# Both attentions of a two-layer vision tower: value products of two key tiles at a time, with other PSUM banks, drains and clears around them

## The reference, cut to what matters

```python
# layer 0: relu attention, causal
scores = jnp.einsum('bhqd,bhkd->bhqk', q, k) / jnp.sqrt(jnp.float32(D))
causal = jnp.tril(jnp.ones((s, s), jnp.float32))
att = jax.nn.relu(scores) * causal
att = att / (jnp.sum(att, axis=-1, keepdims=True) + 1e-09)
ctx = jnp.einsum('bhqk,bhkd->bhqd', att, v)
...
# layer 1: softmax attention, beside the experts
attn = jnp.einsum('bqhd,bkhd->bhqk', q, k) / jnp.sqrt(jnp.asarray(hd, x.dtype))
attn = jax.nn.softmax(attn, axis=-1)
attn_out = jnp.einsum('bhqk,bkhd->bqhd', attn, v).reshape(B, S, D)
...
return attn_out + moe_out
```

## Time and profile before

| | us |
|---|---|
| runs, median (lowest to highest) | 2062.03 (2059.68 to 2064.87) |
| the profiled execution, its own time | 2057.7 |
| its span | 2055.7 |
| causal attention | 324 to 519 |
| experts' last result to the next stage's first DVE instruction | 1562.3 to 1572.9 |
| softmax attention, first maximum to end | 1574.4 to 2055.7 |
| busy: PE, DVE, ACT, POOL | 1875.9, 1491.7, 937.9, 981.3 |

### The profile page before, as it was taken

The page is one execution under the profiler, slowest core; times in us unless marked ns, Lnnn a source line. Parts: engine busy times, 40 slices in busy tenths (PEclk is TensorE's granted clock), DMA queues, the critical chain, the costliest instruction groups (busy, mean ns, idle before and its releaser), DMA issues. The chain is left out here.

```text
span 2055.7 us, 36446 instructions
## 1 busy us (share of the span) xinstructions
PE 1875.9 (91%) x10746; PEld 1173.4 (57%) x10746; DVE 1491.7 (73%) x4145; ACT 937.9 (46%) x2116; POOL 981.3 (48%) x1657
## 2 busy tenths in 40 slices
PE   6997998999899999799998798799797999999997
PEld 5885773333688888577776332688573233333332
DVE  3334896777477777699997587677666889988981
ACT  1112564556122212444443344455451477777777
POOL 3554564555333333233332111388545666666662
PEclk9998998999899999999999898799997799999999
DMA  4331668786100000893000200277765444443320
GB/s 136 116 115 32 166 168 205 153 169 126 47 1 1 1 1 1 326 413 158 1 1 3 65 10 11 60 183 197 205 209 141 94 97 100 100 104 92 91 60 27
DMA packets 241226, 215.01 MB, mean 105 GB/s; under 512 B 117210, under 2 KB 215548, under 8 KB 240924
## 3 DMA queue, kind: packets, MB, share of 16 engines
q1 hardware_dynamic: 231404, 186.56, 34.3%
q0 software_dynamic: 9648, 26.36, 4.0%
HBM read 108.04 MB, written 103.12 MB: 103 GB/s over the span
## 5 line engine op out<-in xcount | busy, mean ns | idle before, releaser
L3051 DVE TENSOR_REDUCE attend_mx<-ps 128x1 f32<-128x512 f32 x512 | 321.0, 681 | 37.0 <-PE ps L2705 33.2
L2848 ACT ACTIVATE attend_w<-ps 128x512 f32<-128x512 f32 x512 | 280.6, 597 | 95.0 <-PE ps L2719 87.3
L2705 PE MATMUL ps<-keep_x,keep_o 96*128 96x512 bf16 x512 | 209.0, 414 | 6.3 <-DVE attend_mx L3051 4.5
L2719 PE MATMUL ps<-keep_o,keep_x 99*128 99x512 bf16 x512 | 191.5, 383 | 2.7 <-ACT attend_w L2848 2.7
L2705 PEld LDWEIGHTS ps<-keep_x,keep_o 96*128 96x128 bf16 x512 | 50.1, 98 | 192.2 <-DVE attend_mx L3051 145.5
L981 POOL TENSOR_TENSOR keep_early<-keep_early,first_causal 128x128 f32<-128x128 f32 x256 | 113.3, 458 | 86.0 <-ACT keep_early L949 85.0
L1003 DVE SCALAR_TENSOR_TENSOR keep_early<-ps,first_causal 128x512 f32<-128x512 f32 (+3 forms) x256 | 113.8, 485 | 47.4 <-PE ps L885 43.1
L949 ACT ACTIVATE keep_early<-ps 128x512 f32<-128x512 f32 (+3 forms) x256 | 98.7, 437 | 85.1 <-PE ps L885 84.9
L1216 PE MATMUL ps<-mlp_zT,keep_early 128*128 128x128 f32 x1056 | 129.2, 282 | 8.0 <-ACT mlp_zT L1258 8.0
L2737 PE MATMUL ps<-attend_w,keep_early 128*17 128x512 f32 x1024 | 135.5, 598 | 0.0
L1216 PEld LDWEIGHTS ps<-mlp_zT,keep_early 128*128 128x128 f32 x1056 | 122.9, 195 | 16.0 <-ACT mlp_zT L1258 16.0
(11 more groups left out here) (399 smaller groups left out, 4406.7 us busy)
## 6 DMA issues: line engine op xcount, KB each, us to landing
sorted<-keep_x SPq DMA_DIRECT2D x3, 14720.0 KB, 75.1
tok_xin<-in_xk SPq DMA_DIRECT2D x64, 256.0 KB, 2.6
qk_parts<-qkv_parts SPq DMA_DIRECT2D x33, 384.0 KB, 3.2
qk_parts<-moe_parts SPq DMA_DIRECT2D x32, 384.0 KB
sorted<-moe_zn POOLq DMA_DIRECT2D x69, 128.0 KB, 2.5
keep_o<-qk_parts SPq DMA_DIRECT2D x16, 384.0 KB, 4.5
keep_x<-qk_parts SPq DMA_DIRECT2D x16, 384.0 KB, 5.6
moe_zs<-sorted SPq DMA_DIRECT2D x45, 128.0 KB, 2.5
```

The costliest lines, as they stand in the source:

```text
L2705: nc.tensor.matmul(ps[:, MX + i % RING, :], qs[0:R, x.buf(0), h, t * P:(t + 1) * P], ks[0:R, x.buf(0), h, :], start=True, stop=True).then_ ...
L2719: nc.tensor.matmul(ps[:, SC + i % RING, :], ks[:, x.buf(2), HG * g + j, kt * P:(kt + 1) * P], qs[:, x.buf(2), HG * g + j, :], start=True, ...
L2848: nc.scalar.activation(w[:, j, kt % 2, :], ps[:, SC + (HG * k + j) % RING, :], ACT.Exp)\
L3051: nc.vector.tensor_reduce(mx[:, t, k:k + 1], ps[:, MX + (TB * k + t) % RING, :], AX, ALU.max)\
```

## The change

- *Causal attention.* `w` holds all four key tiles of a unit. The scores rotate through five banks (0, 1, 2, 3, 7) instead of one per head, so a product waits for the reader of the product five before. On PE a unit now is: scores 0, class values, transposes of the unit two before, scores 1, values 2 and 3 of the unit before, scores 2, scores 3, values 0 and 1. ACT takes the context after its weights of tile 1, DVE divides (now one multiplication of 256 columns in place of four of 64) after its weights of tile 1, for the unit two before.
- *Softmax attention.* `w` has four places. Values of steps k-2 and k-1 stand together before the pair j=3 of each even step k. In slots 0 and 1 the maxima use six banks, and one reduction covers two of them. The last addition to `h` is done by DVE instead of POOL.
- *Experts.* SP stores the last 10 results instead of 4, and the wait for them stands in the next pass, on SP ahead of `class_rows`, on ACT and on POOL.
- *Clears.* Six areas before the experts, and the last pass, no longer clear their semaphores and have no second barrier; three later clears and the final one take them over.

```diff
     def clear(self):
-        if self.used:
-            self.nc.clear_and_free_semaphores(self.used)
+        if self.owes is not None:
+            self.owes += self.used
+        elif self.used:
+            self.nc.clear_and_free_semaphores(self.used + list(self.owed))
...
             self.nc.all_engine_barrier()
...
+        BANKS = (0, 1, 2, 3, 7)
+        def bank_of(q, j):
+            return BANKS[(HG * q + j) % len(BANKS)]
...
-                    past(pe, s_p[j] if j % 2 else s_relu[j], q)
-                    nc.tensor.matmul(ps[:, j, kt * P:S], halves[half].ks[:, hh + j, kt * P:(kt + 1) * P],
+                    last_q, last_j = divmod(HG * q + j - len(BANKS), HG)
+                    past(pe, s_p[last_j] if last_j % 2 else s_relu[last_j], last_q + 1)
+                    nc.tensor.matmul(ps[:, bank_of(q, j), kt * P:S], halves[half].ks[:, hh + j, kt * P:(kt + 1) * P],
...
+            for n in range(NG * B):
+                b, g = n // NG, n % NG
+                scores(b, g, 0)
+                class_value(b, g)
+                if n >= 2:
+                    turn(n - 2)
+                scores(b, g, 1)
+                if n >= 1:
+                    values((n - 1) // NG, (n - 1) % NG, 2)
+                    values((n - 1) // NG, (n - 1) % NG, 3)
+                scores(b, g, 2)
+                scores(b, g, 3)
+                values(b, g, 0)
+                values(b, g, 1)
...
+            for n in range(NG * B):
+                weigh(n // NG, n % NG, 0)
+                weigh(n // NG, n % NG, 1)
+                if n >= 1:
+                    take((n - 1) // NG, (n - 1) % NG)
+                weigh(n // NG, n % NG, 2)
+                weigh(n // NG, n % NG, 3)
...
-    LAST = 4
+    LAST = LAST_BLOCKS
...
-                sp.dma_start(io["sorted"][bass.ds(row, P), :], y[j % NY]).then_inc(s_last, 16)
-            sp.wait_ge(s_last, 16 * LAST)
+                sp.dma_start(io["sorted"][bass.ds(row, P), :], y[j % NY]).then_inc(env.s_last, 16)
...
+                        if j == 1 and k % TB == 2 and x.has(2):
+                            class_values(x.n(2), x.b(2), x.half(2), k - 2)
-                        if j == 3:
+                        if j == 3 and k % 2 == 0:
                             if k and x.has(2):
+                                values(x.n(2), x.half(2), x.buf(2), k - 2)
                                 values(x.n(2), x.half(2), x.buf(2), k - 1)
...
+                        if x.s < 2:
+                            if t % 2:
+                                dve.wait_ge(s_msc, MAXIMA * x.n(0) + at + 1)
+                                bank = (MAXIMA * x.s + at - 1) % (2 * RING)
+                                nc.vector.tensor_reduce(mx[:, t - 1:t + 1, k], ps[:, bank:bank + 2, :], AX, ALU.max).then_inc(s_mx, 2)
...
-            end = Slot(UNITS - 1)
-            add(2 * UNITS - 1, 1, end.b(0), 2 * end.half(0) + 1)
...
+            nc.vector.tensor_tensor(hs, hs, o[:, 1, :, :], ALU.add).then_inc(s_o, 1)
```

More of the change, by code:

```diff
@@ L793, with __init__ @@
 class Causal:
-    def __init__(self, nc):
-        self.area = Area(nc, "first")
+    def __init__(self, nc, env):
+        self.area = Area(nc, "first", owed=env.owed)
         self.s_stacks, self.s_values, self.s_cls = (self.area.sems(n, 2) for n in ("stacks", "values", "cls"))
@@ L829, in pass_causal @@
 def pass_causal(nc, env, io):
-    a = Area(nc, "causal")
+    a = Area(nc, "causal", owes=env.owed)
     ps = env.ps
@@ L915, in turn @@
                 for t in range(TB):
-                    last = nc.tensor.transpose(ps[:, 6, t * P:(t + 1) * P], ctx[:, g % 2, t * P:(t + 1) * P],
+                    last = nc.tensor.transpose(ps[:, 6, t * P:(t + 1) * P], ctx[:, n % 2, t * P:(t + 1) * P],
                                                env.ident[:, :])
                 last.then_inc(s_t, 1)
[L920 to L940, removed]
+            for n in range(NG * B):
[12 more added lines that the diff above has]
+                values(b, g, 1)
+            values(B - 1, NG - 1, 2)
+            values(B - 1, NG - 1, 3)
+            turn(NG * B - 2)
+            turn(NG * B - 1)
         @block.scalar
@@ L1013, in divide @@
                 ch.link(nc.vector.reciprocal(den[:, 1, :, :], den[:, 0, :, :]))
[L1014 to L1033 removed]
+                o = env.o[:, 1 + TB * b:1 + TB * (b + 1), HG * HD * g:HG * HD * (g + 1)]
+                nc.vector.tensor_tensor(o.rearrange("p t (j d) -> p t j d", d=HD), sums[:, :, :, 0:HD],
+                                        den[:, 1, :, :].rearrange("p t (j a) -> p t j a", a=1)
+                                        .to_broadcast([P, TB, HG, HD]), ALU.mult).then_inc(s_o, 1)
+            for n in range(NG * B):
+                weigh(n // NG, n % NG, 0)
+                weigh(n // NG, n % NG, 1)
+                if n >= 2:
+                    divide((n - 2) // NG, (n - 2) % NG)
+                weigh(n // NG, n % NG, 2)
+                weigh(n // NG, n % NG, 3)
+            divide(B - 1, NG - 2)
             divide(B - 1, NG - 1)
@@ L1933, in pass_experts @@
             a.sem(n) for n in ("lgs", "chosens", "count", "places", "all", "n", "c_g", "c_p", "c_n"))
-        s_slots, s_dT, s_dz, s_dW, s_dM, s_y, s_last = (a.sem(n) for n in ("slots", "dT", "dz", "dW", "dM", "ys", "last"))
+        s_slots, s_dT, s_dz, s_dW, s_dM, s_y = (a.sem(n) for n in ("slots", "dT", "dz", "dW", "dM", "ys"))
         s_out, s_vout, s_scat, s_zs, s_yout = (a.sems("out", NQ), a.sems("vout", NV), a.sems("scat", NZ), a.sems("zin", NY),
@@ L2703, in max_scores @@
                     pe.wait_ge(s_load[x.buf(0)], LOADED * (x.turn(0) + 1))
-                past(pe, s_mx, MAXIMA * x.n(0) + (i - RING + 1 if i >= RING else (-1, 0, 0)[i]))
-                nc.tensor.matmul(ps[:, MX + i % RING, :], qs[0:R, x.buf(0), h, t * P:(t + 1) * P], ks[0:R, x.buf(0), h, :],
+                if x.s < 2:
+                    at = MAXIMA * x.s + i
+                    past(pe, s_mx, (at - 2 * RING) // 2 * 2 + 2)
+                    bank = at % (2 * RING)
+                else:
+                    first = (60, 60, 64) if x.s == 2 else [MAXIMA * x.n(0) + n for n in (-1, 0, -2)]
+                    past(pe, s_mx, MAXIMA * x.n(0) + i - RING + 1 if i >= RING else first[i])
+                    bank = MX + (i + 1) % RING
+                nc.tensor.matmul(ps[:, bank, :], qs[0:R, x.buf(0), h, t * P:(t + 1) * P], ks[0:R, x.buf(0), h, :],
                                  start=True, stop=True).then_inc(s_msc, 1)
@@ L2803, in _ @@
             end = Slot(UNITS - 1)
+            values(end.n(0), end.half(0), end.buf(0), STEPS - 2)
             values(end.n(0), end.half(0), end.buf(0), STEPS - 1)
@@ L3069, in build @@
         env = Lasting()
+        env.keep, env.owed = keep, []
         env.h = keep.sb("h", [P, NT, D])
@@ L3128, in build @@
             if step is pass_qkv:
-                env.causal = Causal(nc)
+                env.causal = Causal(nc, env)
                 with env.causal.area.ctx:
```

107 lines of the change are left out of this document (47 added, 60 removed).

## The result

The changed kernel takes 2085.46 us (median of 4 runs, 2083.15 to 2090.52), the kernel before 2063.45 beside it (2059.68 to 2066.41, the three runs shown earlier among them). The ratio is 1.0113, 95% interval 1.0095 to 1.0131: slower by 22 us between the medians, 23 by the ratio, where +13 was forecast. The profiled spans are 2055.7 and 2082.7, 27.0 apart, since the profiled execution of before (2057.7) lies 5.8 under its median and that of the changed kernel (2084.51) 0.9; a table of the traces comes to more than the medians by that.

What follows compares the result with a forecast made beforehand. PE was taken to bound the causal attention, DVE mostly the softmax attention. Terms +11, +0.6, +11, +3, -3, -4.7, -3.0 and -1.9 gave +13 us on the 2062.0 median: 2075 us, range 2066 to 2086.

Steps and rivals of the forecast that it cites:

- 5.48 + 0.8: Causal attention: unit of 5.48 us after two saved excursions, plus 0.8 us of PE waiting at scores 3.
- the term of slots 2 to 15: Softmax attention: value bursts cost +0.8 us per slot over 14 slots, +11; bounds -12 and +32.
- the first part: Softmax slots 2 to 15: DVE idle 2.9 us per slot at bursts against 2.37 before, +0.5.
- Slots 16 and 17: Softmax slots without reductions, set by ACT: more idle ahead of exponentials, +3 us; bounds 0 and +5.
- The rest: Slots 0 and 1, both stage ends and the clears together: -3, -4.7, -3.0 and -1.9 us.
- the experts' end: End of experts: POOL's drain hidden, SP's ten stores from 1555.3 end near 1566.7; -4.7 us, bounds 0 and -7.2.
- The seams: Clears between stages: six go for -2.2 us, longer later ones give back 0.3; -1.9, bounds 0 and -3.
- Slots 0 and 1: Softmax start: two-bank maxima save -2.1 us, -3 in all with six banks carrying DVE; bounds 0 and -9.
- case D: Stage ends: gains fail because POOL's drains last as long or SP's stores are late; +8, 2083 us, chance 0.09.
- A: Both attentions gain: waits hidden, DVE never dry, saved excursions give 0.43 us per causal unit; 2024 us, chance 0.16.
- B: One attention gains, the other loses as forecast; 2050 or 2049 us, up to 2066, chance 0.17.
- E: Softmax attention: every burst finds DVE dry, 2.3 us per slot in place of 0.8; +21, 2096 us, chance 0.11.

Runs made afterwards that it cites:

- experiment 3: Changed kernel with two causal attention moves: ACT takes the context after its tile 2 weights, DVE divides after its tile 3 weights; 2077.56 us.
- experiment 2: Changed kernel, bursts kept, two softmax side pieces moved: class token's own part on DVE one reduction earlier, PE's step 2 transposes one pair later; 2063.70 us.
- 8: Changed kernel, bursts kept, with only the class token's own part on DVE one reduction earlier; 2071.14 us.
- experiment 7: Changed kernel with the old causal attention and the old per-step softmax value products, keeping the other parts of the change; 2047.25 us.
- experiment 4: Changed kernel with ACT's context copy and DVE's division later, and PE's transposes between scores 2 and scores 3 in the causal attention; 2066.87 us.

## Why the forecast was right in its direction and short in its size

*The causal attention was right in its mechanism.* The forecast laid out 5.48 + 0.8 and the trace has 5.43 + 0.75; the wait stands inside scores 3 as said. The share is not as said: most of it (0.57) is the second product behind ACT, 0.18 the third behind DVE; the working had DVE as the later one, and experiment 3 cannot separate them. The unit gives 7.6 us over the 28 that are like this one. That the stretch comes to +10.1, near the forecast's +11.6, is in part luck, since 2.0 more were not in the working: where the first half's stacks are loaded for the second sequence, PE waited 0.41 before and now 2.12 and 0.29.

```profile
352.00 1.04 PE L901 MATMUL ps<-first_qs,first_ks 96*128 96x512 bf16 x4 [2.12 <-DMA first_ks<-qk_parts]
353.33 0.39 PE L911 MATMUL ps<-first_cls,first_vb 96*128 96x512 bf16 x1 [0.29 <-DMA first_v<-v_all]
```

*The step that failed is the term of slots 2 to 15*, "+0.8 per slot, 14 slots, +11". It is +1.65 per slot, 29.02 on the mean from 1638.05 to 2015.31 (the same thirteen slots) against 27.37, and +23.5 in all with 2.1 on the way into slot 2. Of its two parts the second was the mis-sized one, "PE will wait at transposes and class values for side copies that DVE makes later, where I put +0.3, an estimate that no row gives". Experiments 2 and 8 measure it: 1.35 per slot. A row did give it: on PE's timeline of the kernel before, shown above, one value block stands between the class product and the transposes that reuse its bank, and what it covered (0.98) was to be read there. Beside it the first part, DVE dry at bursts less what PE saves, was put at +0.5 and is +0.22 (27.59 against 27.37), so a part that was too high hid some of the one that was too low. The rows of experiment 2 bear the 0.22 out: in its 11.9 slots DVE stands 27.3 us ahead of the reductions and 3.5 ahead of the class token's part (L3024), 2.59 per slot for 2.37 before. The 0.86 that PE saves per slot is not seen in the slot; PE stands 1.3 per slot ahead of maxima (15.9 us) instead.

```profile
L3073 DVE TENSOR_REDUCE attend_mx<-ps 128x1 f32<-128x512 f32 x381 | 238.5, 680 | 27.3 <-PE ps L2718 25.6
L3024 DVE TENSOR_TENSOR attend_t<-ps,keep_early 8x136 f32<-8x136 f32 x12 | 3.4, 287 | 3.5 <-PE ps L2790 3.2 <-issue 0.3
```

*Slots 16 and 17* took +6.2 where 3 was put, with a bound of +5: a bound that was too near. Experiment 2 has 58.4 for the stretch of the table (54.4 before, 60.6 after), so 2.2 of it are side pieces too and 4.0 the bursts, inside the bound.

*The rest*, -12.6 in the forecast, is -13.6 by experiment 7, and that the sum fits so well is luck: its parts were off both ways. Inside it the experts' end was too high (-4.7, measured -2.6): SP's ten stores begin when its own loads are through, at 1563.62, which is 1557.6 on the clock of before, not 1555.3. The seams gave more, -4.0 for -1.9; which of the clears gave it no experiment separates. Slots 0 and 1 gave the -3.7, but 2.1 of it come back on the way from `largest` of slot 1 to the class product of slot 2 (18.6 us before, 20.7 in the changed kernel and in experiment 7), which the forecast did not have. The drains behaved as laid out: 6.69 and 6.25 us long, now early enough to be hidden, so the first half of case D fell; its second half, SP's stores being late, came for 2.1 us. Two-bank reductions take 1.13 each (18.19/16), 0.07 less than two of 0.60.

*The rivals.* A was wrong for this kernel and right on the price: its 0.43 per unit appears in full once the cover is there (experiment 4): 5.91 less 5.44 is 0.47 for two excursions. The Trainium skill, TensorEngine Tiling (Array Packing), Key Properties, says that a change of tiling mode drains the engine, and this trace agrees with it. B did not come. E, every burst finds DVE dry, came in its sign and not in its size: in the slot shown DVE stands 0.65, 1.39, 0.90 and 0.58 behind the four bursts, 3.5 us where E had 4.6. But most of this goes with PE's two waits: in experiment 2 two spells are left, 1.39 and some 0.75, which is near the forecast's own picture (2.5 bursts at 1.16).

## What to carry to other kernels

When a block of PE work is moved, list what it stood between, not only what it is: each bank that one side of it fills and the other reuses loses the block's length as cover (here 0.98 us of cover, of which 0.79 was paid). An order that saves changes of array mode is worth 0.2 us each only if the banks' readers are covered elsewhere; the cheapest cover is other PE work that is due anyway, such as the transposes of 0.44 us that turned 5.88 into 5.44. And an estimate that "no row gives" should widen the range by the longest block that is taken away, for each place.

## What the runs showed of the hardware

A faster causal attention ran into its loads. In experiment 4 PE stood 3.27 us for the same stacks, and behind it the granted clock was at half for some 7 us: a set of four products of 512 columns takes 1.68 (351.68 to 353.36) where it takes 0.87 at 425.54, which are the levels of 1.2 and 2.4 GHz. The windows (PE, PEld, DVE, ACT, POOL; then clock, DMA share, GB/s):

```profile
351.68 1.89 PE L901 MATMUL ps<-first_qs,first_ks 96*128 96x512 bf16 x4 [3.27 <-DMA first_ks<-qk_parts]
353.36 0.63 PE L911 MATMUL ps<-first_cls,first_vb 96*128 96x512 bf16 x1
```

```profile
345.00:350.00 5.00, 3.41 (x44) 1.64 (x36) 2.76 (x9) 1.71 (x6) 2.54 (x6) 1.00 1.18 211
350.00:355.00 5.00, 3.32 (x9) 1.20 (x9) 1.71 (x3) 1.69 (x4) 0.99 (x3) 0.63 1.11 215
355.00:360.00 5.00, 5.00 (x45) 2.50 (x44) 2.89 (x9) 2.18 (x6) 2.60 (x6) 0.68 0.79 171
360.00:365.00 5.00, 5.00 (x53) 2.62 (x53) 3.90 (x11) 3.39 (x9) 3.11 (x8) 1.00 0.02 5
```

The two units there (from 342.90 and from 351.68) take 8.78 and 8.51 where the others take 5.44: 6.4 us together, 3.3 in the one that ends with the wait and 3.1 in the one at the lower clock. In the changed kernel the wait of 2.12 us at the same place left the clock at 1.00. Whether an earlier load would give these us back was not tried.
